# Differential attention of a fused block: another order of the same work on four engines, and nine products of zeros an iteration

## The reference

```
q, k = rotary(query @ Wq), rotary(query @ Wk)         # 2H halves of width D = 16
v    = (query @ Wv).reshape(bsz, T, H, 2, D)
s    = where(causal, einsum('bthd,bshd->bhts', q_a, k_a) * D**-0.5, -1e30)      # a = 1, 2
attn_a = softmax(s) @ [v1, v2]
attn = attn_1 - lambda_full * attn_2                  # then a filter over time, RMS norm, @ Wout
```

## Time and profile before

| what | us |
|---|---|
| median of 3 runs | 4687.87 (4680.11 to 4709.7) |
| the profiled execution, its own time | 4695.65 |
| its span | 4694.0 |
| differential attention, first product to last | about 2142 to 2937, some 795 |
| one iteration there (rows below) | 47.65 |
| TensorE busy in the span | 3781.9 (81%) |
| VectorE busy in the span | 2264.4 (48%) |

### The profile page before, as it was taken

How to read it: one execution, slowest core, us unless ns; L and a number is a source line. 1 busy time by engine, 2 the same in 40 slices (tenths; PEclk the granted TensorE clock), 3 DMA queues, 4 the chain that set the end, 5 groups by cost and what they waited for, 6 DMA issues and landing times. The chain is left out here.

```text
span 4694.0 us, 167100 instructions
## 1 busy us (share of the span) xinstructions
PE 3781.9 (81%) x68160; PEld 2478.8 (53%) x68160; DVE 2264.4 (48%) x6301; ACT 1351.7 (29%) x4238; POOL 553.6 (12%) x1085
## 2 busy tenths in 40 slices
PE   7788888888888888887888887577999879488830
PEld 3377777777777777774333332333333344244410
DVE  2155555555555555554666665133666633121124
ACT  1033333333333333333444443122444411011100
POOL 0000000000000000001222222000000014200034
PEclk9999999999999999998898898688999989798865
DMA  2140000000000000002110100201111021387756
GB/s 68 34 163 0 0 0 0 0 0 0 0 0 0 0 0 0 0 0 69 32 47 31 47 31 1 83 18 48 63 54 56 31 79 42 131 261 240 244 159 155
DMA packets 144487, 256.69 MB, mean 55 GB/s; under 512 B 25943, under 2 KB 76247, under 8 KB 142388
## 3 DMA queue, kind: packets, MB, share of 16 engines
q1 hardware_dynamic: 118388, 201.90, 13.2%
q0 software_dynamic: 21248, 53.30, 4.1%
q10 hardware_dynamic: 4800, 0.81, 0.1%
HBM read 147.89 MB, written 62.92 MB: 45 GB/s over the span
## 5 line engine op out<-in xcount | busy, mean ns | idle before, releaser
L305 PE MATMUL gru_pr<-gru_whh,h 128*4 128x128 f32 x16384 | 544.3, 274 | 230.5 <-DVE h L396 230.5
L305 PEld LDWEIGHTS gru_pr<-gru_whh,h 128*4 128x4 f32 x16384 | 388.7, 87 | 373.9 <-DVE h L396 367.7
L305 PE MATMUL gru_pz<-gru_whh,h 128*4 128x128 f32 x16384 | 542.3, 273 | 1.5 <-issue 1.5
L305 PE MATMUL gru_pn<-gru_whh,h 128*32 128x128 f32 x16384 | 542.8, 273 | 0.0
L305 PEld LDWEIGHTS gru_pn<-gru_whh,h 128*32 128x32 f32 x16384 | 459.3, 110 | 1.3
L305 PEld LDWEIGHTS gru_pz<-gru_whh,h 128*4 128x4 f32 x16384 | 438.9, 87 | 10.0 <-issue 1.7
L376 DVE STREAM_TRANSPOSE gru_tr<-gru_pr 128x128 f32<-128x128 f32 x512 | 162.2, 317 | 380.2 <-PE gru_pr L305 380.2
L340 ACT ACTIVATE gru_rn<-gru_pre 128x16 f32<-128x16 f32 x512 | 118.4, 231 | 707.5 <-DVE gru_pre L378 707.5
L859 DVE TENSOR_REDUCE da_mx<-da_ps 128x2 f32<-128x256 f32 (+3 forms) x256 | 201.3, 818 | 237.0 <-PE da_ps L569 237.0
L280 POOL COPY gru_pick<-ident 128x4 f32 x512 | 96.4, 188 | 1688.7 <-PE gru_pz L296 1683.2
L389 DVE STREAM_TRANSPOSE gru_tz<-gru_pz 128x64 f32<-128x64 f32 x1024 | 194.7, 229 | 121.7 <-PE gru_pz L305 121.7
(11 more groups left out here) (262 smaller groups left out, 5516.5 us busy)
## 6 DMA issues: line engine op xcount, KB each, us to landing
ex_wg<-in_L_ffn_gate_up_proj SPq DMA_DIRECT2D x64, 768.0 KB, 5.4
ex_wd<-in_L_ffn_down_proj SPq DMA_DIRECT2D x64, 384.0 KB, 6.2
xg<-gru_zeros SPq DMA_DIRECT2D x4, 4096.0 KB
da_hb<-wide SPq DMA_DIRECT2D x16, 1024.0 KB, 4.7
fa_hb<-xnT SPq DMA_DIRECT2D x16, 1024.0 KB
ex_xg<-xg SPq DMA_DIRECT2D x64, 256.0 KB, 2.7
eo<-ex_eo POOLq DMA_DIRECT2D x64, 256.0 KB, 6.3
da_wg<-ahead SPq DMA_DIRECT2D x48, 256.0 KB, 4.8
```

The costliest lines, as they stand in the source:

```text
L305: last = nc.tensor.matmul(rows(j), of(c), whh[:, c, g, j, :], start=(c == 0 and start), stop=(c == KD - 1))
```

## The change

The same results are computed, with the same tiles. What differs:

- `score_for_max` and `maximum` take query tile 3 first and tile 0 last (`i = TT - 1 - m`): falling.
- `sum_exponentials` stands behind the first `score_keys` of a slot, not ahead of it, and ScalarE copies the sums between the two parts of the first exponential.
- k is projected, copied, swapped and rotated in slot a = 1 for the group two ahead, where before the projection stood at that slot's end and the rest in the next slot a = 0. v is projected in step 3 of slot a = 1 and behind it, and copied by ScalarE at the start of the next iteration. q is projected in two parts in slot a = 0.
- The reciprocals and `weighted` stand near the ends of the slots: VectorE has `weighted` and `difference` behind the last `accumulate` of the slot. `output` moves from slot a = 0, step 2, to the start of slot a = 1, ahead of `weigh_values`.
- `add_nothing` adds nine products an iteration, of two new tiles of zeros (bf16, 128 x 128 against 128 x 512), onto the accumulating bank of the weighted values.

```diff
+            def add_nothing(a, n):
+                for _ in range(n):
+                    nc.tensor.matmul(ps[:, WORK[a], :], still[:], stillr[:], start=False, stop=False)
...
             def score_for_max(u, m, par, a, alone=False, start=False):
-                i = m
+                i = TT - 1 - m
...
                 maxima_to_rows(s, 0, start=first)
-                if not last:
-                    swap_pairs(1, it * 2 + 3)
                 if not first:
+                    add_nothing(1, 2)
                     weigh_values(s - 1, TT - 1, nxt, 1)
+                score_keys(s, 0, par, 0, start=first)
+                if not first:
                     sum_exponentials(s - 1, 1)
-                score_keys(s, 0, par, 0, start=first)
+                score_for_max(s + 1, 1, par, 1)
...
+                maxima_to_rows(s, 1)
                 if not first:
...
                     output(it - 1)
-                score_for_max(s + 1, 3, par, 1)
-                weigh_values(s, 2, par, 0)
-                score_keys(s, 3, par, 0)
...
                 weigh_values(s - 1, TT - 1, par, 0)
+                score_keys(s, 0, par, 1, alone=last)
                 sum_exponentials(s - 1, 0)
-                score_keys(s, 0, par, 1, alone=last)
...
# VectorE, iteration
+                maximum(s + 1, 2, 1)
+                accumulate(s, 1)
                 if not last:
                     times_sine(0, it * 2 + 4)
+                    rotate(0, it * 2 + 4)
+                maximum(s + 1, 3, 1)
+                maxima_spread(s + 1, 1)
+                accumulate(s, 2)
                 if not first:
                     weighted(s - 1, 1)
                     difference(it - 1)
-                maximum(s + 1, 2, 1)
-                if not last:
-                    rotate(0, it * 2 + 4)
-                accumulate(s, 1)
-                maximum(s + 1, 3, 1)
-                maxima_spread(s + 1, 1)
-                accumulate(s, 2)
...
                 accumulate(s, 0)
-                weighted(s - 1, 0)
...
                 accumulate(s, 2)
+                weighted(s - 1, 0)
```

More of the change, by code:

```diff
@@ L633, in iteration @@
                         pe.wait_ge(sum_kept, s)
-                    project(nxt, 0, range(KD))
-                score_for_max(s + 1, 1, par, 1)
+                    project(nxt, 0, (0, 1))
                 pe.wait_ge(v_ready, it + 1)
-                if not last:
-                    pe.wait_ge(sined, it * 2 + 3)
                 weigh_values(s, 0, par, 0)
@@ L645, in iteration @@
                 score_keys(s, 2, par, 0)
+                if not last:
+                    swap_pairs(0, it * 2 + 4)
+                add_nothing(0, 2)
+                score_for_max(s + 1, 3, par, 1)
+                weigh_values(s, 2, par, 0)
+                score_keys(s, 3, par, 0)
+                add_nothing(0, 3)
+                s = it * 2 + 1
+                if not last:
+                    score_for_max(s + 1, 0, nxt, 0)
+                maxima_to_rows(s, 1)
                 if not first:
@@ L685, in iteration @@
                 score_keys(s, 3, par, 1, alone=last)
-                if k_follows(p, o):
-                    project(par, 1, (2, 3))
+                if not last:
+                    project_v(nxt, (2, 3))
             loaded(0, 0, 0)
@@ L768, in keep_output, with exponentials @@
                                      ps[:, WORK[1], :].rearrange("p (i f) -> p i f", f=P), ACT.Copy).then_inc(a_written, 1)
-            def exponentials(s, n):
-                if not isinstance(s, int) or s or n >= 2:
+            def exponentials(s, n, parts=(0, 1)):
+                if parts[0] == 0 and (not isinstance(s, int) or s or n >= 2):
                     act.wait_ge(product, s * TT + (n - 1))
                     act.wait_ge(added, s * TT + (n - 1))
-                for part in range(2):
+                for part in parts:
                     act.wait_ge(keys_scored, s * 8 + (2 * n + part + 1))
@@ L782, in iteration @@
                 s = it * 2
-                if not last:
[L785 to L789, removed]
+                if not first:
+                    keep_v(it, par)
+                    keep_products(s - 1, 1, it - 1)
+                exponentials(s, 0, (0,))
+                if not first:
+                    keep_sums(s - 1, 1)
+                exponentials(s, 0, (1,))
+                if not last:
+                    halves_of_keys(it + 1, nxt)
+                exponentials(s, 1)
+                if not last:
+                    keep_raw(0, it * 2 + 4, it * 2 + 3)
+                exponentials(s, 2)
                 if not first:
@@ L792, in iteration @@
                 if not last:
-                    keep_raw(0, it * 2 + 4, it * 2 + 3)
-                    halves_of_keys(it + 1, nxt)
+                    halves_of_q(it + 1, nxt, (0,))
+                exponentials(s, 3)
+                if not last:
+                    halves_of_q(it + 1, nxt, (1,))
+                s = it * 2 + 1
+                if not first:
+                    keep_output(it - 1)
+                keep_products(s - 1, 0, it)
+                exponentials(s, 0, (0,))
+                keep_sums(s - 1, 0)
+                exponentials(s, 0, (1,))
+                if k_follows(p, o):
+                    keep_raw(1, it * 2 + 5, it * 2 + 4)
                 exponentials(s, 1)
                 exponentials(s, 2)
[L797 to L806, removed]
                 reciprocal(s - 1)
[L808 to L811, removed]
                 exponentials(s, 3)
@@ L949, in _ @@
             maxima_spread(0, 0)
+            times_sine(1, 3)
+            rotate(1, 3)
             over_iterations(dve, iteration)
```

63 lines of the change are left out of this document (35 added, 28 removed).

## The result

| | before | changed |
|---|---|---|
| median of 7 runs each, us | 4697.28 (4680.11 to 4709.7) | 4666.53 (4653.76 to 4691.09) |
| ratio, 95% interval | | 0.995 (0.9929 to 0.9971) |
| span of the profiled execution, us | 4694.0 | 4659.9 |
| one iteration in its trace, us | 47.65 | 46.13 |
| mean granted clock over iterations 1 to 14 | 0.90 | 0.95 |

The forecast was 4679, a gain of 9 us; the ratio makes it 23. The interval of the ratio lies wholly under 1, and the change is less than 1%.

A forecast was written before the change was run, and what follows sets the result against it. TensorE was taken to bound the stage by work, waits and clock together. An iteration of 39.3 work, 5.7 waits and 2.05 low clock makes 47.05 us against 47.65, 9 us over 15 iterations: 4679 us, range 4640 to 4722.

The forecast's parts named there:

- The waits of the new order: TensorE's idle times over both slots, walked along VectorE's queue: 5.7 us an iteration, against 6.4 before.
- The sum at full clock: One iteration without any low clock: 39.3 us of TensorE work and 5.7 of waits, 45.0 us.
- What bounds the kernel: TensorE bounds the stage, by its work (37.3 us an iteration), its waits (6.4) and its clock (3.9) together.
- The price of the low clock: In the kernel before, 9.5 us an iteration at 1.2 GHz cost 3.9 us, 0.41 us for each.
- the clock after: Cost of low clock in the changed kernel: 4.75 us at 0.43 each, 2.05 us an iteration.
- one fall an iteration: Granted clock drops once, at the start of slot a = 1, instead of twice; 45% chance, 4670 to 4692 us.
- The last iteration: Iteration that keeps its chain; with the prologue's extra waits set at nothing, within 5 us either way.
- The clock staying up: Rival: no drop to the low clock in the stage, 45.0 us an iteration, 4648 us; 15% chance.
- Two falls: Rival: the clock also drops at the start of slot a = 0; 49.1 us an iteration, 4710 us; 25% chance.
- its deciding point: Whether the 1.3 us wait at slot a = 0's start counts like the 0.5 to 0.8 waits that felled the clock.
- waits vanish altogether: Rival: VectorE's tail overlaps better, slot a = 1's 3.4 us vanish, clock holds; 41.6 us an iteration, 4597 us; 10% chance.
- falling tiles leave the work of a slot as it is: Query tile order changes no work in a slot, only what the first key scores wait for.

The follow-up runs named there:

- the kernel before with zeros: Twelve products of zeros an iteration added to the unchanged earlier kernel, in its waits: ratio 0.9889 to that kernel, 44.46 us an iteration, clock 1.00.
- rising tiles: Changed kernel with query tile 0 first again in scores and maxima: ratio 1.0039 to the kernel before, 49.90 us an iteration, clock 0.93.
- the repeat: Changed kernel as it is, run again on another group's chip: ratio 0.9956 to the kernel before, 46.13 us an iteration, clock 0.95.

## Why the prediction was right, and what was off

**The waits of the new order** were right, each in its place: 1.3 us forecast and 1.36 measured ahead of the key scores of slot a = 0; 0.15 and 0.18 ahead of the second scores; 0.5 and 0.35 in step 3; 2.1 and 1.90 ahead of `output`; 1.3 and 1.21 (1.17 to 1.45 over the iterations) behind it. Slot a = 0 was to take 20.0 us and takes 19.9. Each came from following VectorE's queue in order from one known end, with distances between starts as durations.

**The sum at full clock** was 45.0 and is 44.4 and 44.8 in the two iterations where the clock held, 44.5 over all 14. The work is as forecast, 39.3 and 39.4 (iteration 1); the 0.5 is in the waits. Zeros cost 0.25 each from start to start (three in 0.75 at 2508.59), 0.22 was taken.

**What bounds the kernel** was right: work, waits and clock together. That the waits hardly shrink and that the gain must be the clock's was right as well, and the kernel before with zeros shows it. The price of the low clock there was 3.9 by my count of work, and is 3.2.

**The term that was mis-sized is the clock after.** I took one fall an iteration, worth 4.75 us x 0.43 = 2.05. It is one fall, at slot a = 1, with a mean clock of 0.95 as forecast, but in 12 of 14 iterations, and it costs less: slot a = 1 takes 26.91 us at clock 0.87 and 24.58 at 1.00, 2.33 for some 7.0 us at the low level, 0.33 each and not 0.43. Part of the low stretch lies over the wait behind `output`, where nothing is lost. The old slot a = 1, from which I took the price, has less than 0.5 us of waiting behind its fall, as the sums there start soon after the window that shows 0.58:

```profile
2482.65 1.93 PE L606 MATMUL da_ps<-da_total,da_ones 128*32 128x512 f32 x8 [0.79 <-ACT da_pv L749]
```

The mean over the iterations is 1.6. With the 0.5 in the full-clock sum this makes 46.13 in place of 47.05, 14 us over 15 iterations. The gain that I forecast, 0.6 us an iteration, is smaller than these two errors together; that both lie on the same side, and the forecast gain on the right side of nothing, is in part luck.

**The last iteration**, set at nothing within 5, gave 5.8; no run takes that apart.

**The rivals.** The clock staying up (15%) is what iterations 0 to 2 did. Two falls (25%) came when all nine zeros were taken out, two of them ahead of the first key scores of slot a = 0, at the place that I had named, so its deciding point was right: 1.80 us of waiting fells the clock there, 1.36 with zeros ahead does not. No run takes out these two alone. The stretch ahead of that wait holds four transposes. The Trainium skill's rule, in "TensorE: Matmul & The Clock Gate", Part 4, that transposes do not count as busy in the same way would fit this; no run took transposes away from there with the waits as they are, so it stays open. That waits vanish altogether (10%) did not happen, and needed another order.

**One thing the prediction passed over.** It said that falling tiles leave the work of a slot as it is. That is so, but they are worth 3.8 us an iteration in this order, 2.7 of it waiting, and I costed them only at the slot's start, not at its end.

## What to carry to other kernels

Before reordering for waits, read how much of the time is spent at the low clock, and ask for each wait whether it is long enough to fell it: filling the waits at two places with products of zeros gained twice what a full reorder did, and it is also the quickest test of that price. Then look at what the late engine does ahead of the one result that is waited for; moving four VectorE instructions and one accumulation behind it made the waits short enough to do without zeros, but for one low stretch in 14 iterations. A wait that is removed by moving its cause can come back where the cause is queued next, as 2.07 us did as 1.90 ahead of `output`, and can be found by following that engine's queue.

## What the runs showed of the hardware

Products of a tile of zeros hold the granted clock: 1.00 with them in the waits of the kernel before, 0.90 without. At the slot starts it held through waits of 1.19 us without zeros and 1.36 behind two zeros; it fell at 1.79 and 1.80 with none right ahead, but for once each, and at 2.21 behind two zeros (rising tiles) in 6 of 14 iterations. So the same wait can go either way: 1.45 us behind `output` felled the clock in 3 of 14 iterations once the wait ahead of it was filled, and the changed kernel's 1.90 and 1.44 together did not in iteration 2, but in all later ones. Whole iterations repeat to 0.01 us from the first runs to the repeat (46.13 twice), while the median of the same kernel moved from 4666.5 to 4704.3; in the two traces 30 of 33 us of this lie in the stages behind.
